# First attention of a two-layer block: v computed feature-major in fp32r, centred by its mean, and divided on token-major data

## The reference, cut to what matters

```python
def mala_attn(q, k, v):            # q, k, v: [B,S,H=8,16]
    q = q * cos + rotate_half(q) * sin
    k = k * cos + rotate_half(k) * sin
    kv = jnp.einsum('bshd,bshe->bhde', k, v)
    ksum = k.sum(axis=1)
    vsum = v.sum(axis=1)
    num = jnp.einsum('bshd,bhde->bshe', q, kv) * scale + vsum[:, None, :, :]
    den = jnp.einsum('bshd,bhd->bsh', q, ksum) * scale + seq_len
    return num / den[..., None]
o = mala_attn(q, k, v) + lepe_conv(v, lepe_w, lepe_b)     # 5 taps along the sequence, per feature
o = o.reshape(Bb, Ss, H * DV) * o_gate
return o @ Wo.T
```

## Time and profile before

| | us |
|---|---|
| median of three runs | 746.12 |
| the profiled execution | 746.4 |
| its span, first to last instruction | 744.6 |
| PE busy | 683.6 (92%) |
| DVE busy | 591.7 (79%) |
| ACT busy | 445.6 (60%) |
| POOL busy | 403.9 (54%) |
| granted PE clock, mean of the span | 0.96 |
| bytes moved | 12.50 MB, 17 GB/s in the mean |

### The profile page before, as it was taken

The page is one execution under the profiler, slowest core; times in us unless marked ns, Lnnn a source line. Parts: engine busy times, 40 slices in busy tenths (PEclk is TensorE's granted clock), DMA queues, the critical chain, the costliest instruction groups (busy, mean ns, idle before and its releaser), DMA issues.

```text
span 744.6 us, 13318 instructions
## 1 busy us (share of the span) xinstructions
PE 683.6 (92%) x3798; PEld 531.5 (71%) x3798; DVE 591.7 (79%) x1855; ACT 445.6 (60%) x850; POOL 403.9 (54%) x857
## 2 busy tenths in 40 slices
PE   4566769999999999999999999999999999999994
PEld 3455658787878778777878787777877787766652
DVE  2463768989988888889888888789898888888672
ACT  2323447667667667666766667566676667666421
POOL 2244555454647474856646474946646474734522
PEclk9665989999999999999999999999999999999997
DMA  6000000000101010000101010000101000000000
GB/s 219 15 0 15 1 15 1 8 7 2 29 1 29 2 29 2 1 29 0 29 0 29 0 28 0 4 26 0 29 0 29 0 14 0 16 0 15 10 19 15
DMA packets 18677, 12.50 MB, mean 17 GB/s; under 512 B 704, under 2 KB 18240, under 8 KB 18368
## 3 DMA queue, kind: packets, MB, share of 16 engines
q1 hardware_dynamic: 18624, 11.95, 5.3%
HBM read 7.75 MB, written 4.19 MB: 16 GB/s over the span
## 4 chain that ended last, share of the span: by engine, by line
PE 39%; POOL 27%; issue 23%; DVE 6%; ACT 2%; POOLq 1%; DMA 1%; SPq 0%; DVEq 0%; ACTq 0%
POOL moment L1154 8%; PE bank L556 7%; POOL rstd L1154 5%; PE bank L356 4%; PE bank L347 4%; PE bank L349 4%; PE bank L348 4%; POOL qk L1134 3%; POOL centered L1199 2%; POOL x0T_lo L1184 2%; PE bank L469 1%; POOL x3T_lo L1189 1%; POOL x_b L1179 1%; POOL x L1193 1%; POOL x L1195 1%
## 5 line engine op out<-in xcount | busy, mean ns | idle before, releaser
L347 PE MATMUL bank<-x3T_hi,w_hi 128*128 128x512 f32 x288 | 146.8, 510 | 4.5 <-DVE gu L1044 4.5
L556 PE MATMUL bank<-hid,whole 128*128 128x512 f32 x288 | 147.9, 595 | 1.0 <-DVE hid L1047 1.0
L730 ACT ACTIVATE silu<-bank 128x512 f32<-128x512 f32 x144 | 85.6, 595 | 70.0 <-PE bank L349 68.3
L349 PE MATMUL bank<-x3T_hi,w_lo 128*128 128x512 f32 x288 | 113.7, 395 | 0.0
L348 PE MATMUL bank<-x3T_lo,w_hi 128*128 128x512 f32 x288 | 113.5, 394 | 0.0
L1044 DVE TENSOR_TENSOR gu<-silu,bank 128x512 f32<-128x512 f32 x128 | 87.3, 682 | 24.3 <-PE bank L349 22.0
L1054 DVE TENSOR_TENSOR hid<-gu,bank 128x512 f32<-128x512 f32 x128 | 87.5, 684 | 2.1 <-DVE gu L1044 0.2
L1141 POOL TENSOR_TENSOR rden_x<-rden,whole 128x512 f32<-128x512 f32 x16 | 17.4, 1086 | 128.6 <-DVE rden L844 128.6
L1154 POOL TENSOR_TENSOR moment<-stats 128x4 f32<-128x4 f32 x192 | 41.3, 247 | 84.3 <-DVE stats L860 84.3
L1134 POOL TENSOR_TENSOR qk<-rope_c,rope_s 128x512 f32<-128x512 f32 x32 | 40.5, 1278 | 71.3 <-DVE rope_s L831 71.3
L347 PEld LDWEIGHTS bank<-x3T_hi,w_hi 128*128 128x128 f32 x288 | 54.4, 189 | 31.2 <-issue 13.6
(11 more groups left out here) (203 smaller groups left out, 1724.0 us busy)
## 6 DMA issues: line engine op xcount, KB each, us to landing
x_in<-x SPq DMA_DIRECT2D x16, 256.0 KB, 3.0
out<-x SPq DMA_DIRECT2D x16, 256.0 KB, 2.3
whole<-w_whole SPq DMA_DIRECT2D x1, 1198.5 KB, 5.5
w_raw<-w SPq DMA_DIRECT2D x1, 1152.0 KB
w_raw<-w SPq DMA_DIRECT2D x1, 546.0 KB, 6.8
whole<-w_whole SPq DMA_DIRECT2D x16, 32.0 KB
whole<-w_whole SPq DMA_DIRECT2D x1, 64.0 KB
```

The source lines that it names most:

```text
L347: mm(out, wh, mh, start=True, stop=False)
L349: return mm(out, wl, mh, start=False, stop=True)
L556: mm(YB[:], whole[:, a:a + P], hid[:, c % 2], start=c == 0, stop=c == CHUNKS).then_inc(p_w2.sem, 1)
L730: fn(silu[:, c % 2], GB[:], ACT.Silu).then_inc(a_silu.sem, 1)
```

## The change

What it does, by engine. PE: v is made feature-major from the split block, three fp32r products of 512 columns, in place of four fp32 products of 128; the transposes of v now go the other way and come from `v_cent`; denominator and numerator are one product each tile, token-major, with 136 columns (128 of the numerator and 8 of the denominator); the transposes of `rden_x` become transposes of `att`. ACT: sums v, makes minus the mean, subtracts it (`v_cent`), and no longer copies the numerator. DVE: masks numerator and denominator part in one operation, divides on token-major data (`att`), and adds mean and convolution (`mixT`); in stage b two additions of a bias become one. POOL: `rden_x` and `mixT` are gone, the multiplication with the gate (`oT`) has come to it from DVE. The turn lists of PE, ACT, DVE and POOL are all written anew.

```diff
-W_LATE, W_SPLIT = WEIGHT_COLS["w3"][1], WEIGHT_COLS["g"][1]
+W_LATE, W_SPLIT = WEIGHT_COLS["w3"][1], WEIGHT_COLS["v"][1]
...
-            def a_v_(n):
-                pe.wait_ge(a_xT[0].sem, a_xT[0].at(n))
+            def a_vT_(n):
+                pe.wait_ge(g_x0l.sem, g_x0l.at(n))
                 if started(n):
                     pe.wait_ge(v_res[0].sem, v_res[0].at(n - 1))
-                for t in range(TILES):
-                    last = mm(tile(A1, t), tile(xT[0], t), raw("v"), start=True, stop=True)
-                last.then_inc(p_v.sem, 1)
+                mm3(A1[:], hi("v"), lo("v"), x0T_hi[:], x0T_lo[:]).then_inc(p_vT.sem, 1)
...
-            def a_vT_(n):
-                pe.wait_ge(a_v.sem, a_v.at(n))
+            def a_v_(n):
+                pe.wait_ge(a_cent.sem, a_cent.at(n))
                 pe.wait_ge(v_rope.sem, v_rope.at(n))
-                transpose_tiles(A1, lambda t: v_one[:, t, 0:P], ident).then_inc(p_vT.sem, 1)
+                transpose_tiles(A1, lambda t: tile(v_cent, t), ident).then_inc(p_v.sem, 1)
...
-            def a_den(n):
+            def a_num_(n):
                 pe.wait_ge(a_qT.sem, a_qT.at(n))
                 pe.wait_ge(v_kv.sem, v_kv.at(n))
-                for t in range(TILES):
-                    last = mm(A1[:, t * HEADS:(t + 1) * HEADS], tile(qT, t), ks_m[:, t // 2, :], start=True, stop=True)
-                last.then_inc(p_den.sem, 1)
-            def a_num_(n):
-                for s in range(SEQS):
-                    last = mm(A0[:, s * SEQ:(s + 1) * SEQ], kv_m[:, s, :], qT[:, s * SEQ:(s + 1) * SEQ], start=True, stop=True)
-                last.then_inc(p_num.sem, 1)
-            def a_rd(n):
-                pe.wait_ge(g_rd.sem, g_rd.at(n))
-                transpose_tiles(A1, lambda t: rden_x[:, t], ident).then_inc(p_rd.sem, 1)
+                for s, b in ((0, A0), (1, A1)):
+                    for i in range(2):
+                        last = mm(b[:, i * SEQ:i * SEQ + KV], tile(qT, 2 * s + i), kv_m[:, s, :], start=True, stop=True)
+                    last.then_inc(p_num.sem, 1)
+            def a_aT(n):
+                pe.wait_ge(v_att.sem, v_att.at(n))
+                transpose_tiles(A0, lambda t: att[:, t], ident).then_inc(p_aT.sem, 1)
...
+                fn(neg_mean[:], v_sum[:], ACT.Copy, scale=-1.0 / SEQ).then_inc(a_mean.sem, 1)
+                act.wait_ge(a_mean.sem, a_mean.at(n))
+                for s in range(SEQS):
+                    fn(v_cent[:, s * SEQ:(s + 1) * SEQ], vT[:, s, 2:2 + SEQ], ACT.Identity,
+                       bias=neg_mean[:, s:s + 1]).then_inc(a_cent.sem, 1)
-            def a_numv(n):
...
             def a_att(n):
-                tt(attT[:], numT[:], A1[:], ALU.mult).then_inc(v_att.sem, 1)
-            def a_gate(n):
-                tt(oT[:], mixT[:], gT[:], ALU.mult).then_inc(v_oT.sem, 1)
+                for s, b in ((0, A0), (1, A1)):
+                    each = rden[:, 2 * s:2 * s + 2].unsqueeze(3).broadcast_to([P, 2, HEADS, HD])
+                    tt(att[:, 2 * s:2 * s + 2].rearrange("p t (h d) -> p t h d", d=HD),
+                       by_tile(b)[:, :, 0:P].rearrange("p t (h d) -> p t h d", d=HD), each, ALU.mult).then_inc(v_att.sem, 1)
+            def a_mix(n):
+                for s in range(SEQS):
+                    stt(mixT[:, s * SEQ:(s + 1) * SEQ], A0[:, s * SEQ:(s + 1) * SEQ], neg_mean[:, s:s + 1], conv[:, s],
+                        ALU.subtract, ALU.add).then_inc(v_mix.sem, 1)
...
@@ DVE turn @@
+                if b: a_layer_norm(i - 1)
                 if e: d_res(i - 4, odd)
-                if b: a_layer_norm(i - 1)
...
@@ POOL turn @@
                 if a: x0_lo(i)
+                if e: ln_of(3, i - 4)
                 if a: a_rope(i)
...
-                if a: a_rd(i)
+                if b: ln_of(1, i - 1)
                 if c: x3_lo(i - 2, odd)
-                if b: ln_of(1, i - 1)
-                if a: a_mix(i)
-                if e: ln_of(3, i - 4)
+                if a: a_gate(i)
+                if e: e_norm(i - 4)
```

More of the change, by code:

```diff
@@ L45 @@
 UNITS = P // EXPERTS
+KV = P + HEADS
+LOGITS = PROJ + len(RANKS)
 ALLCH = CHUNKS + 1
@@ L185, in build @@
         qk = sb("qk", [P, TILES, 2 * P])
-        v_one = sb("v_one", [P, TILES, P + 1])
+        v_one = sb("v_one", [P, TILES, KV])
         gT = sb("gT", [P, BLOCK])
-        kv_m = sb("kv_m", [P, SEQS, P])
-        ks_m = sb("ks_m", [P, SEQS, HEADS])
+        kv_m = sb("kv_m", [P, SEQS, KV])
         v_sum = sb("v_sum", [P, SEQS])
+        neg_mean = sb("neg_mean", [P, SEQS])
+        v_cent = sb("v_cent", [P, BLOCK])
         qT = sb("qT", [P, BLOCK])
@@ L193, in build @@
         conv = sb("conv", [P, SEQS, SEQ])
-        den = sb("den", [P, TILES * HEADS])
+        den = sb("den", [P, TILES, HEADS])
         rden = sb("rden", [P, TILES, HEADS])
-        rden_x = sb("rden_x", [P, TILES, P])
-        numT = sb("numT", [P, BLOCK])
-        attT = sb("attT", [P, BLOCK])
+        att = sb("att", [P, TILES, P])
         mixT = sb("mixT", [P, BLOCK])
@@ L567, in turn @@
                 if d: d_cT(i - 3)
-                if a: a_v_(i)
                 if e: d_yT(i - 4)
+                if a: a_vT_(i)
                 if d: d_hidden(i - 3, 1 - odd, 1)
@@ L574, in turn @@
                 if b: b_xT(i - 1)
+                if d: d_down(i - 3, 0)
                 if a: a_g_(i)
-                if d: d_down(i - 3, 0)
                 if b: b_small(i - 1)
+                if a: a_v_(i)
                 if d: d_hidden(i - 3, 1 - odd, 2)
-                if a: a_vT_(i)
+                if a: a_kv(i)
+                if a: a_qT_(i)
                 if d: d_down(i - 3, 1)
@@ L582, in turn @@
                 if d: d_down(i - 3, 2)
-                if a: a_kv(i)
-                if a: a_qT_(i)
+                if c: r_xT(i - 2, odd)
                 if d: d_hidden(i - 3, 1 - odd, 4)
-                if a: a_den(i)
-                if c: r_xT(i - 2, odd)
+                if a: a_num_(i)
+                if c: r_gate(i - 2)
                 if d: d_down(i - 3, 3)
-                if a: a_num_(i)
+                if b: b_dnT(i - 1)
                 if d: d_hidden(i - 3, 1 - odd, 5)
-                if c: r_gate(i - 2)
-                if b: b_dnT(i - 1)
                 if d: d_down(i - 3, 4)
@@ L835, in a_kv @@
                 kv = A1[:].rearrange("p (s c) -> p s c", s=SEQS)
-                tt(kv_m[:], kv[:, :, 0:P], const("hmask").unsqueeze(1).broadcast_to([P, SEQS, P]), ALU.mult).then_inc(v_kv.sem, 1)
-                tt(ks_m[:], kv[:, :, P:P + 1].broadcast_to([P, SEQS, HEADS]),
-                   const("hmask8").unsqueeze(1).broadcast_to([P, SEQS, HEADS]), ALU.mult).then_inc(v_kv.sem, 1)
+                first, end = CONST_COLS["hmask"][0], CONST_COLS["hmask8"][1]
+                mask = whole[:, first:end].unsqueeze(1).broadcast_to([P, SEQS, KV])
@@ L1135, in a_rope, with a_gate @@
                        ALU.add).then_inc(g_qk.sem, 1)
-            def a_rd(n):
-                pool.wait_ge(v_rden.sem, v_rden.at(n))
-                heads = rden[:].rearrange("p t h -> p (t h)").unsqueeze(2).broadcast_to([P, TILES * HEADS, HD])
-                ones = const("ones")[:, 0:HD].unsqueeze(1).broadcast_to([P, TILES * HEADS, HD])
-                tt(rden_x[:].rearrange("p t (h d) -> p (t h) d", d=HD), heads, ones, ALU.mult).then_inc(g_rd.sem, 1)
-            def a_mix(n):
-                pool.wait_ge(v_att.sem, v_att.at(n))
-                pool.wait_ge(v_conv.sem, v_conv.at(n))
-                tt(mixT[:], attT[:], conv[:].rearrange("p s l -> p (s l)"), ALU.add).then_inc(g_mix.sem, 1)
+            def a_gate(n):
+                pool.wait_ge(v_mix.sem, v_mix.at(n))
+                pool.wait_ge(a_g.sem, a_g.at(n))
+                tt(oT[:], mixT[:], gT[:], ALU.mult).then_inc(g_oT.sem, 1)
             def ln_of(k, n):
```

132 lines of the change are left out of this document (65 added, 67 removed).

## The result

The changed kernel took 775.79 us, the median of four runs (775.1 to 777.42), against 745.58 for the kernel before (743.97 to 746.69) beside it: ratio 1.0413, 95% interval 1.0397 to 1.043. It is slower by 4.1%. Slower was the forecast's sign; its size, 752, and its range up to 761 were wrong. The profiled execution took 775.5 us, its span 773.7, 29 more than before.

The account below looks back on a forecast made before the run. PE's list bounds the middle; less PE work would leave it waiting for `x3` and `oT`. Twelve turns +6.6, turn 3 -0.7, turns 0 to 2 -1.5, turns 16 and 17 +1: +5.4, so 752 us; range 736 to 761.

Parts of the forecast that it names:

- Cheap things: DVE's and ACT's lists: DVE's gains and losses within 0.2 us; late ACT copies absorbed, or up to 0.3 a turn.
- the chain to `x3`: POOL's last norm through `x3`: ready at 20.0 us behind chunk 0, 20.65 with contention; PE there at 19.2.
- this term, 0.65: Contention on POOL: convolution tap 2 on DVE lengthens the second operation on `x3` by 0.65 us, bounds 0 and 0.74 + 0.5.
- forecast 0.8 to 1.5: Sign in the profile: PE idle ahead of `r_xT`, released by POOL's second operation on `x3`, 0.8 to 1.5 us a turn.
- The end of stage a: `oT`, now on POOL, ready about when PE wants it, 16.3 us; wait put at 0.3, bounds 0 and 0.6.
- wrong in kind if the wait before `a_out` is the larger one: Sign against the forecast: PE waits longer before stage a's output product than ahead of `r_xT`.
- PE's own work, -0.88 a turn: PE's list gets shorter through v, denominator and numerator: 40.0 us a turn in place of 40.92 if nothing stops PE.
- the second rival: `x3` never stops PE, so the full -0.88 us counts in 13 turns: 733.5 us; chance 0.13.
- +0.08: PE's new numerator product with denominator columns takes 0.95 us with start-up in place of the numerator's 0.87.
- The third (760): Tap 1 also hits and late `oT` delays `x0T_lo` and v; decides beyond a microsecond late; some 1.2 a turn; chance 0.15.
- +0.53 and +0.57: Growth of a pass's second turn (40.92 to 41.45 us) and first turn (42.14 to 42.71), across the loop's branch.

Follow-up runs that it names:

- thin_pool: Changed kernel with four POOL operations (gate, centered, x4, x2's bias) on 8 of 512 columns, leaving out most of their work: 745.6 us, ratio 1.001.
- ln3_idle: Changed kernel with only the last norm moved on POOL, into its 10.8 us wait for the statistics of b: 772.8 us, ratio 1.0355.
- calm: Changed kernel, POOL's last norm in its wait for b's statistics; centered, x4, x2's bias behind next x0T_lo, x4 after x1's normalisation: 752.0 us, ratio 1.0092.
- ln3_back: Changed kernel with POOL's old order: last norm behind the gate, centered and x4 behind norm 0; other engines' lists stay changed: 758.9 us, ratio 1.0189.

## Why the prediction was wrong, point by point

- **The step that failed** is in "Cheap things": DVE "within 0.2, in a list that waits for PE elsewhere". DVE's list grew by 3.0 us a turn in `r_groups(4)` and by about 1.0 in `lg` and `lg_s` (713 and 790 ns for 250 and 263), and its idle time of 8.3 us a pair was not enough. The first part is what costs the time: thin_pool keeps the second (716 and 790 ns) and has a pair of 82.5. A mechanism was missed, not a size: I counted DVE's instructions, not what POOL runs beside them. That the sign came out right was mostly luck: it rested on the chain to `x3`, which accounts for about 3 of the 30 us.
- **Contention in one direction only.** The prediction took from the earlier trace rows that POOL stands while DVE streams, and charged it to `x3`. The second operation on `x3` stayed at 1.04, which the text had named as the sign that this term, 0.65, was wrong. It was not tested in this place: tap 2 started at 474.00, behind the end of that operation at 473.45, because `lg_s` ahead of it had waited for the same operation (0.88 for 0.17). Tap 1 did lengthen the operation ahead of `x3`, `proj_rn`, to 1.38, so the form does contend. The other direction, DVE waiting for POOL, was in the text only as "beside it DVE runs small routing operations with two SBUF inputs", and there it was feared for `oT`, which kept its 1.27.
- **The chain to `x3`**: forecast 20.0 without contention; measured 20.27 behind chunk 0 (473.45 - 453.18), of which 0.37 is `proj_rn` beside tap 1. Right within 0.1 without it. PE stood 0.73 ahead of `r_xT` (473.50, less 471.91 for the start of the `d_down` ahead of it and 0.86 for this; 0.55 of it is shown as idle), forecast 0.8 to 1.5. But ln3_idle, which takes the last norm off this chain, gained only 3 us, with the wait ahead of `r_xT` gone in one turn of two (0.55 in the other).
- **The end of stage a**: the wait ahead of `a_out` was forecast at 0.3 and is about 0.1; "wrong in kind if the wait before `a_out` is the larger one" looked 3 us too early. The larger wait was the last `d_down` product, which no term had.
- **PE's own work, -0.88 a turn**: too large. Where nothing stops PE, in calm, a turn takes 40.8 against 41.1 before; the stages of thin_pool give 40.49 us of busy PE in a turn of 41.04, those of before 41.00 of 41.00. That is -0.35 to -0.5, so even the second rival, 733.5, was out of reach. Two terms can be named: the new v product takes 0.80 start to start (446.64 - 445.84 in calm) where 0.70 was set, and the old numerator took 0.68 (460.98 - 460.30, to the row of the next product), not 0.87, while the new one takes 0.92 (476.31 - 475.39): +0.24 for the forecast's +0.08. The rest is open.
- **Rivals.** The third (760) had the right sign and "`x0T_lo` and v then come late" for a mechanism, which ln3_back shows (1.41 us of PE); in the changed kernel neither that wait nor a late `oT`, its trigger, happened.
- **The loop's branch**: both turn types were forecast to grow alike, +0.53 and +0.57. They grew by 1.7 and about 2.6; the difference fits DVE's idle time at the branch, which lies bare once DVE is the bound, but no run tests it alone.

## What to carry to other kernels

Before moving a step between or along the lists of VectorE and GpSimd, write down which operations will run side by side, and count for each long GpSimd operation what is left of it on the VectorE operation that reads only SBUF and starts during it, however small that is (reductions kept their time here). Put GpSimd's long operations where VectorE reads PSUM; that, with the last norm in POOL's idle time, brought 775.8 down to 752.0 with nothing left out. Cutting them may help too, but was run only with most of the columns left out. And when a bound engine waits for another in one place, look at the idle time of that other engine over a whole turn before moving the place: moving the wait alone gave nothing.

## What the runs showed of the hardware that was not expected

- The engine that came second lost what was left of the other's operation less about 0.14 us, in both directions: DVE's 0.22 us became 1.24 with 1.17 to go (64 elements behind a POOL operation of 512), POOL's `proj_rn` 1.01 became 1.38 with 0.52 of a tap to go, and in the kernel before `centered` 1.04 became 1.58 with 0.68 of `comb` to go.
- Not only two inputs from SBUF: tensor_scalar (penalty 175 to 599 ns, the normalisation of x1 1.10 to 2.91 us) and the cast (223 to 839 ns) waited too. Products with one input in PSUM (`gu`, `hid`) kept 675 to 688 ns in the mean in every kernel, the statistics 0.87 us, and the reduction `g_rank` 220 ns, also where it ran in the middle of `x4`.
- With short operations of 0.20 us, nearly the same stretch of POOL cost DVE next to nothing (r4 1.9 for 4.6), with most of the columns left out.
